# Tokens kept in float32 until they are turned, and cut into halves as the turned bank is emptied

## What is computed

```python
x = x + _L0_gnn_ref(_layernorm(x), adj, L0_gnn_W, L0_gnn_a)
x = x + _L0_ffn_ref(_layernorm(x), router_w, w1, b1, w2, b2)   # gelu, hidden 256
x = x + _L1_gnn_ref(_layernorm(x), adj, L1_gnn_W, L1_gnn_a)
x = x + _L1_ffn_ref(_layernorm(x), Wg, bg, bias, W1, b1, W2, b2)  # relu, hidden 512
# an expert layer: logits = t @ router; the best 2 of 8 experts; their weights w
# out = sum over the two of w_e * (act(t @ w1[e] + b1[e]) @ w2[e] + b2[e])  (layer 0 adds t)
```

## Time and profile before

| | us |
|---|---|
| median of 3 runs | 1315.85 (1315.29 to 1318.03) |
| the profiled execution | 1316.0 |
| its span, first to last instruction | 1314.2 |
| TensorE busy (products) | 1061.2, 81% |
| VectorE busy | 956.5, 73% |
| GpSimd busy | 706.3, 54% |
| ScalarE busy | 545.9, 42% |
| mean granted clock of TensorE | 0.882 |

### The profile page before, as it was taken

How to read it: one execution, slowest core, us unless ns; L and a number is a source line. 1 busy time by engine, 2 the same in 40 slices (tenths; PEclk the granted TensorE clock), 3 DMA queues, 4 the chain that set the end, 5 groups by cost and what they waited for, 6 DMA issues and landing times.

```text
span 1314.2 us, 31672 instructions
## 1 busy us (share of the span) xinstructions
PE 1061.2 (81%) x9392; PEld 888.3 (68%) x9393; DVE 956.5 (73%) x1904; ACT 545.9 (42%) x1223; POOL 706.3 (54%) x752
## 2 busy tenths in 40 slices
PE   6999765369999993477777587579999999899995
PEld 4777554258888883356555373368989987788984
DVE  5888898966777774469899787947766765666673
ACT  3666564912222221577777584112222232122221
POOL 4567657036666653778772281045443206777773
PEclk9999865569999997788879757689999999999998
DMA  9311233025555553336543464447776625444450
GB/s 284 79 49 41 81 113 128 1 65 163 165 161 166 166 160 119 92 104 171 151 137 104 138 200 119 28 131 221 205 223 183 173 78 155 126 136 134 139 144 21
DMA packets 126096, 172.53 MB, mean 131 GB/s; under 512 B 35109, under 2 KB 94000, under 8 KB 125744
## 3 DMA queue, kind: packets, MB, share of 16 engines
q0 software_dynamic: 28288, 83.03, 23.7%
q1 hardware_dynamic: 89504, 88.22, 21.3%
q10 hardware_dynamic: 8208, 0.07, 1.0%
HBM read 100.87 MB, written 71.44 MB: 131 GB/s over the span
## 4 chain that ended last, share of the span: by engine, by line
PE 48%; issue 18%; DVE 12%; POOL 12%; DMA 5%; ACT 3%; POOLq 0%; DVEq 0%; SPq 0%; ACTq 0%
PE bank L970 19%; PE bank L984 18%; POOL WREG L595 5%; PE bank L953 4%; PE bank L781 3%; DVE X L1306 2%; POOL X L678 2%; POOL WREG L643 2%; DMA WREG<-expert_outputs,pos_both 1%; DVE arena L1653 1%; ACT b_bc L1043 1%; DVE stats L1296 1%; DMA out<-X,scatter_row 1%; DMA X<-first_rows,gather_row 1%; DVE arena L1654 1%
## 5 line engine op out<-in xcount | busy, mean ns | idle before, releaser
L1205 ACT ACTIVATE arena<-bank,b1T 128x256 f32<-128x256 f32 (+1 forms) x464 | 176.4, 457 | 507.9 <-PE bank L970 507.8
L984 PE MATMUL bank<-WREG,arena 128*128 x2544 | 301.3, 273 | 16.4 <-issue 11.5
L970 PE MATMUL bank<-arena,WREG 128*128 128x256 f16 (+1 forms) x2784 | 311.7, 266 | 2.6 <-DVE arena L1717 2.6
L984 PEld LDWEIGHTS bank<-WREG,arena 128*128 128x128 f16 x2544 | 245.6, 98 | 53.0 <-issue 23.4
L970 PEld LDWEIGHTS bank<-arena,WREG 128*128 x2784 | 252.5, 99 | 32.2 <-issue 3.6
L1723 DVE CAST arena<-arena 128x1024 f16<-128x1024 f32 (+1 forms) x140 | 82.2, 587 | 192.1 <-ACT arena L1205 192.1
L667 POOL DMA_INDIRECT arena<-split_tokens,gather_row x136 | 134.9, 992 | 124.7 <-DVE gather_row L1694 47.1
L781 PE MATMUL bank<-wg_sb,arena 128*128 128x258 f32 x512 | 145.0, 433 | 47.2 <-ACT arena L1016 39.9
L595 POOL DMA_INDIRECT WREG<-expert_outputs,pos_both x128 | 127.5, 996 | 64.4 <-issue 36.8
L678 POOL DMA_INDIRECT X<-token_rows,gather_row x72 | 73.3, 1018 | 160.6 <-DMA first_rows<-X 67.4
L781 PEld LDWEIGHTS bank<-wg_sb,arena 128*128 128x128 f32 x512 | 105.6, 215 | 71.4 <-ACT arena L1016 41.7
(11 more groups left out here) (204 smaller groups left out, 1497.6 us busy)
## 6 DMA issues: line engine op xcount, KB each, us to landing
first_rows<-X SPq DMA_DIRECT2D x72, 257.0 KB, 4.3
expert_outputs<-arena SPq DMA_DIRECT2D x68, 256.0 KB
X<-in_x SPq DMA_DIRECT2D x16, 512.0 KB, 6.0
split_tokens<-WREG SPq DMA_DIRECT2D x16, 512.0 KB, 2.9
stage_w<-in_L_ffn_W SPq DMA_DIRECT2D x16, 512.0 KB, 4.8
token_rows<-X SPq DMA_DIRECT2D x8, 1024.0 KB, 7.2
token_rows<-WREG SPq DMA_DIRECT2D x16, 512.0 KB, 3.6
stage_w<-in_L_ffn_w SPq DMA_DIRECT2D x16, 256.0 KB, 2.8
```

The lines of the kernel that those rows point to most:

```text
L970: last = mm(hb, w1_at(L, ea, wh, kc, fc), tT[:, tb:tb + width], start=n == 0, stop=n == 3 * KC - 1)
L984: last = mm(ob[a], hsrc[:, h0:h0 + P], w2_at(L, e[a % len(e)], wh, fc), start=fc == 0 and n == 0, stop=fc == FC - 1 and n == 2)
L1205: ins = A(hid[:, h0:h0 + width], bank[2 + 2 * (u % 2) + fc // 2][:, b0:b0 + width], ACT.Gelu if L == 0 else ACT.Relu, bias=cut(b1T, ea * F ...
```

## The change

- `y32` is now 16 tiles long and takes the place of `y16`. Of each pair ScalarE scales the first tile (`normalise`) and VectorE the second (`cut_tokens`, a tensor_scalar). Nothing is cast or subtracted before the turn; GpSimd's loop is gone.
- SyncE stores `y32` itself. The bytes of a token are the same, 1024.
- TensorE turns four float32 blocks of 128 by 128 for a pair, and for a slot of the experts, in place of eight half-precision ones. They fill the bank with 512 float32 columns.
- ScalarE casts the bank to the upper part (512 columns), VectorE subtracts this from the bank for the lower part: `high_tokens` and `cut_tokens` in the token stage, `high_turned` and `low_turned` in the experts. `copy_yT` and `copy_T` are gone.
- In the experts' slots ScalarE casts slot s + 3 ahead of activating slot s + 2. Ahead of the loop its order is cast 0, cast 1, activate 0, cast 2, activate 1.
- Products, their order and the layout of `tT` stay; in `yT` only the order of blocks changes.

```diff
@@ buffers
-        y32, yT, y16 = ring0[:, 0:8 * D], ring0[:, 8 * D:12 * D].bitcast(F16), ring0[:, 16 * D:32 * D].bitcast(F16)
+        yT, y32 = ring0[:, 0:4 * D].bitcast(F16), ring0[:, 16 * D:32 * D]
@@ SyncE, stores
-                        sp.wait_ge(yl_ready[L], at(i * 8 + 2 * h + 2))
-                        y4 = y16[:, 4 * h * 512:(4 * h + 4) * 512]
+                        sp.wait_ge(y_ready[L], at(i * 8 + 2 * h + 2))
+                        sp.wait_ge(half_ready[L], at(i * 8 + 2 * h + 2))
+                        y4 = y32[:, 4 * h * D:(4 * h + 4) * D]
@@ GpSimd, the loop of the token stage
-                with pool.Fori(0, TILES // 16) as i:
-                    for q in range(8):
-                        loop_wait(pool, hi_ready[L], at(i * 8 + q + 1))
-                        nc.gpsimd.tensor_tensor(y16_4[:, 2 * q:2 * q + 2, D:2 * D], y32_4[:, 2 * (q % 4):2 * (q % 4) + 2, :],
-                                                y16_4[:, 2 * q:2 * q + 2, 0:D], ALU.subtract).then_inc(yl_ready[L], 1)
@@ TensorE, turn_tokens
-                    pe.wait_ge(yl_ready[L], at(i * 8 + q + 1))
+                    pe.wait_ge(y_ready[L], at(i * 8 + q + 1))
+                    pe.wait_ge(half_ready[L], at(i * 8 + q + 1))
                     yT_copied(pe, L, i, q - 2)
-                    for j in range(8):
-                        last = nc.tensor.transpose(bank[q % 2][:, j * (P // 2):(j + 1) * (P // 2)].bitcast(F16),
-                                                   y16[:, (8 * q + j) * P:(8 * q + j + 1) * P], ident16[:])
+                    for j in range(4):
+                        last = nc.tensor.transpose(bank[q % 2][:, j * P:(j + 1) * P], y32[:, (4 * q + j) * P:(4 * q + j + 1) * P], ident[:])
@@ TensorE, turn_over
-                    for j in range(4):
+                    for kc in range(KC):
                         for a in range(ST):
-                            last = nc.tensor.transpose(bank[u % 2][:, (j * ST + a) * (P // 2):(j * ST + a + 1) * (P // 2)].bitcast(F16),
-                                                       source[a][:, j * P:(j + 1) * P], ident16[:])
+                            last = nc.tensor.transpose(bank[u % 2][:, (kc * ST + a) * P:(kc * ST + a + 1) * P],
+                                                       source[a][:, kc * P:(kc + 1) * P], ident[:])
@@ ScalarE, normalise (one tile in place of two) and the cast
+                    p = i * 8 + q
+                    if q % 2 == 0:
+                        loop_wait(act, y_stored[q // 2][L], 16 + i * 16)
+                    loop_wait(act, yT_mm[L], at(p - 7))
+                    A(y32[:, 2 * q * D:(2 * q + 1) * D], xs(2 * p), ACT.Identity, scale=one("rs2", 2 * p), bias=one("nm2", 2 * p)).then_inc(y_ready[L], 1)
+                def high_tokens(i, q):
+                    p = i * 8 + q
+                    v = q % 2
+                    loop_wait(act, yT_mm[L], at(p + 1))
+                    loop_wait(act, logit_mm[L], at(p - 1))
+                    A(yT[:, v * 1024:v * 1024 + 512], bank[v][:], ACT.Copy).then_inc(yT_high[L], 1)
@@ ScalarE, the loop of the token stage
+                with act.Fori(1, TILES // 16) as i:
+                    for q in range(8):
+                        high_tokens(i, q - 3)
+                        normalise(i, q)
@@ ScalarE, experts
+                def high_turned(s, u):
+                    loop_wait(act, T_mm[L], at(s + 1))
+                    loop_wait(act, h_mm[L], at(s - 1))
+                    A(tT[:, (u % 2) * 4 * SLOT:(u % 2) * 4 * SLOT + KC * SLOT], bank[u % 2][:], ACT.Copy).then_inc(T_high[L], 1)
                 def slot(s, u, i, es):
+                    if u + 3 < SLOTS[L]:
+                        high_turned(s + 3, u + 3)
                     if u + 2 < SLOTS[L]:
                         activate(s + 2, u + 2, es[2])
-                for s in range(2):
-                    activate(s, s, first[s])
+                high_turned(0, 0)
+                high_turned(1, 1)
+                activate(0, 0, first[0])
+                high_turned(2, 2)
+                activate(1, 1, first[1])
@@ VectorE, cut_tokens
-                        loop_wait(dve, y_ready[L], at(p + 1))
-                        V.tensor_copy(y16_4[:, 2 * q:2 * q + 2, 0:D], y32_4[:, 2 * (q % 4):2 * (q % 4) + 2, :]).then_inc(hi_ready[L], 1)
-                    if not (first and q < 2) and (q - 2) % 4 != 3:
-                        loop_wait(dve, yT_mm[L], at(p - 1))
-                        loop_wait(dve, logit_mm[L], at(p - 3))
-                        V.tensor_copy(yT[:, v * 1024:(v + 1) * 1024], bank[v][:].bitcast(F16)).then_inc(yT_ev[L], 1)
+                        t = 2 * p + 1
+                        ts(y32[:, (2 * q + 1) * D:(2 * q + 2) * D], xs(t), one("rs2", t), one("nm2", t), ALU.mult, ALU.add).then_inc(half_ready[L], 1)
+                    if not (first and q < 2):
+                        loop_wait(dve, yT_high[L], at(p - 1))
+                        tt(yT[:, v * 1024 + 512:(v + 1) * 1024], bank[v][:], yT[:, v * 1024:v * 1024 + 512], ALU.subtract).then_inc(yT_ev[L], 1)
@@ VectorE, experts
-                def copy_T(s, u):
-                    loop_wait(dve, T_mm[L], at(s + 1))
-                    loop_wait(dve, h_mm[L], at(s - 1))
-                    V.tensor_copy(tT[:, (u % 2) * 4 * SLOT:(u % 2 + 1) * 4 * SLOT], bank[u % 2][:].bitcast(F16)).then_inc(T_ev[L], 1)
+                def low_turned(s, u):
+                    loop_wait(dve, T_high[L], at(s + 1))
+                    b = (u % 2) * 4 * SLOT
+                    tt(tT[:, b + KC * SLOT:b + 2 * KC * SLOT], bank[u % 2][:], tT[:, b:b + KC * SLOT], ALU.subtract).then_inc(T_ev[L], 1)
```

More of the change, by code:

```diff
@@ L667, in gather @@
                     nc.gpsimd.indirect_dma_start(
-                        out=gat[:, u * 512:(u + 1) * 512], out_offset=None, in_=table,
+                        out=gat[:, u * D:(u + 1) * D], out_offset=None, in_=table,
                         in_offset=bass.IndirectOffsetOnAxis(ap=gather_row[:, t:t + 1], axis=0)).then_inc(gathered[u // ST], 16)
@@ L1093, in normalise @@
                 def normalise(i, q):
-                    p = i * 4 + q
-                    loop_wait(act, yl_ready[L], at(p - 3))
-                    for a in range(2):
-                        t = 2 * p + a
-                        b = (2 * q + a) * D
-                        ins = A(y32[:, b:b + D], xs(t), ACT.Identity, scale=one("rs2", t), bias=one("nm2", t))
-                    ins.then_inc(y_ready[L], 1)
+                    p = i * 8 + q
[9 more added lines that the diff above has]
+                    A(yT[:, v * 1024:v * 1024 + 512], bank[v][:], ACT.Copy).then_inc(yT_high[L], 1)
                 for g in range(GROUPS):
@@ L1137, in _ @@
                         normalise(0, 3)
+                        high_tokens(0, 0)
                     if n < GROUPS and L == 1:
@@ L1146, in _ @@
                         squares(g + 2, 1)
-                def copy_yT(i):
-                    p = i * 4 - 1
-                    loop_wait(act, yT_mm[L], at(p + 1))
-                    loop_wait(act, logit_mm[L], at(p - 1))
-                    A(yT[:, 1024:2048], bank[1][:].bitcast(F16), ACT.Copy).then_inc(yT_act[L], 1)
-                def four_pairs(i):
-                    for q in range(3):
-                        normalise(i, q)
-                    copy_yT(i)
-                    normalise(i, 3)
-                four_pairs(1)
-                act.wait_ge(rs2_ready[L], at(2))
-                with act.Fori(2, TILES // 8) as i:
-                    four_pairs(i)
-                copy_yT(TILES // 8)
+                for q in range(4, 8):
+                    high_tokens(0, q - 3)
+                    normalise(0, q)
+                act.wait_ge(rs2_ready[L], at(2))
+                with act.Fori(1, TILES // 16) as i:
+                    for q in range(8):
+                        high_tokens(i, q - 3)
+                        normalise(i, q)
+                for q in range(-3, 0):
+                    high_tokens(TILES // 16, q)
                 def copy_low(j):
```

51 lines of the change are left out of this document (22 added, 29 removed).

## The result

The changed kernel takes 1319.62 us, the median of 11 runs (1316.91 to 1322.24), against 1315.29 us (1311.22 to 1318.03) for the kernel before in the same session. The ratio is 1.0033, with a 95% interval from 1.0021 to 1.0044. It is slower, by 4.3 us. The profiled execution has a span of 1318.4 us, before it was 1314.2, at a mean granted clock of 0.881 (0.882). One execution each of e3, of e10 and of the kernel before on the slower chip, 1.3 to 2 times as long as the others, stands in no median and no ratio here.

A forecast was written before the change was run, and what follows sets the result against it. TensorE was taken to bound the experts, a ring over two banks the token loop. Terms -2.3 - 0.5 - 1.2 + 1.0 - 1.0 + 2.2 + 1.3 sum to -0.5 us: 1315.4 us, no change, range 1305 to 1321.

The forecast's parts named there:

- The token loop: Token stage, both layers: steps fall from 1.45 and 1.42 us to 1.39, 26 per layer; -2.3 us.
- The ring: Token loop over two banks: turn, cast, subtraction, logits, turn after next; 2.78 us for two steps, 1.39 each.
- the new chain is no shorter: Rival, token loop: longer hand-overs and address issue on VectorE make steps 1.45; 1319.6 us with starts at upper bounds; chance 0.15.
- The scaling on VectorE: Token loop: VectorE's scaling of one tile per pair takes 0.28 us, at most about 0.42.
- The ends: Token loop's first turn after the statistics (-0.48) and last turn's way to the logits (+0.24); -0.5 us for both layers.
- Routing without GpSimd: Layer 0's routing arithmetic, no longer beside GpSimd's one-hot tables and last expert's weights; -1.2 us.
- GpSimd beside the last attention group: Layer 0: moved GpSimd work may delay the last softmax's product; cost between 0 and 1.16, taken as +1.0 us.
- The float32 turn in the experts: Experts' slots: four float32 turns take 0.43 us against 0.45 for eight half-precision ones; taken as -1.0 us.
- The rival of a load for each block: Rival, float32 turn: each block costs a whole load, 141 ns; 1330 us, a third of it 1321; chance 0.15.
- The start of the experts: First output products come later behind ScalarE's order: layer 0 +2.2 (0.6 to 2.9), layer 1 +1.3 us (0.6 to 2.5).
- The clock rival: Rival, token loop: TensorE's clock stays up, step 1.15 us; 1302.9 us, or 1309 in half the loop; chance 0.2.

The follow-up runs named there:

- e3: Changed kernel with ScalarE's first expert activation right behind its first cast and VectorE's first split ahead of its third subtraction; 1393.32 us on a slower chip, ratio 1.0015.
- e10: Changed kernel, still looped, but a turn in TensorE's token loop waits only for the subtraction two pairs back; 1314.19 us, ratio 0.9980.
- e4: Changed kernel with TensorE's token loop written out; 1379.74 us on a slower chip, ratio 0.9937 to the kernel before.
- e6: Kernel before with TensorE's token loop written out and nothing else; 1316.01 us, ratio 1.0003.
- e11: Changed kernel with one more wait, so GpSimd makes layer 0's tables and last weights late, beside routing again; 1322.78 us, ratio 1.0050.
- e9: The changed kernel's experts, float32 table and float32 turn behind the token stage of the kernel before; 1313.40 us, ratio 0.9981.
- e5: The changed kernel itself, run again on a second chip; 1320.32 us, ratio 1.0035 to the kernel before.
- e7: Changed kernel with the start order of e3 and, in layer 0, an early one-column Gelu that loads the table; 1318.19 us, ratio 1.0023.
- e12: Changed kernel with logits two turns behind, the edits of e4 and e10, and the early one-column Gelu of e7; 1294.88 us, ratio 0.9843.
- e8: Changed kernel with logits two turns behind and the edits of e4 and e7; 1311.88 us, ratio 0.9959.

## Why the prediction was wrong

I gave 1315.4 us and called it no change; 1319.6 came, 4.3 slower than before, where I had said that 2.6 can be told apart. It lies inside my range of 1305 to 1321 only because two misses partly cancel: the token loop came 9.5 us above its term, and the experts, +2.5 with their starts, came out at about -2.5. The first miss alone gives 1324.9. That the range held is luck. In the order of its steps:

- **The token loop, -2.3.** This is the step that failed; +7.2 was measured (40.61 - 37.72 + 41.19 - 36.88). The ring was named rightly, and two of its operations were right to 0.01: cast 0.60, subtraction 0.69. The mis-sized terms are TensorE's: 0.28 from the logits to the next turn was 0.44, the turn 1.09 in place of 1.03, and the end of TensorE's loop, 0.50 once in eight steps, was not in the sum at all. The hand-overs were right in sum only, 0.22 for my 0.20: 0.16 behind VectorE and 0.03 behind the two others. Together these make the step 1.52 without the loop's end and 1.56 to 1.58 with it, in place of 1.39. The 0.28 was the shortest such leg of the kernel before, and it holds the products and loads alone. I took for granted that waits already met are free, because in the kernel before they are: they lie under the wait for GpSimd. The change took that cover away and added a wait. e4, e6 and e10 show it from three sides.
- **The rival "the new chain is no shorter"** was the nearest, and had 1319.6 as its time, which is what came. But that is chance. It put the issue on VectorE, and it was TensorE's; the step was 1.56 to 1.58, not 1.45; and the experts paid part of it back, where this rival had their starts at the upper bounds. It had 0.15. The rule I would use now would have given it more: a cycle that was never on the path has unpriced legs.
- **The scaling on VectorE** took 0.41 in the loop, its upper bound of 0.42, not 0.28. It cost nothing in the ring: the subtraction still began 0.03 behind the cast.
- **The ends, -0.5.** The first turn came 1.3 and 1.4 us after the statistics in place of 1.8 and 1.9, as forecast; the last turn's way to VectorE's routing grew by 0.4 in place of 0.24.
- **Routing without GpSimd, -1.2.** Last turn to rank products went from 13.80 to 12.71, the 0.4 above included, so 1.1 net and 1.5 for the arithmetic. e11 puts it back. **GpSimd beside the last attention group, +1.0:** not seen in the loop's start. The softmax product L1379 (L1381 before) took 0.69, as alone, though it began under GpSimd's iota, which has no input and ended 0.29 after the product's start (rows below). By the Trainium skill, SBUF — State Buffer, section "SBUF: two separate sides", the pair of ports is locked against such a VectorE operation only by a GpSimd operation that reads SBUF. The trace agrees with that as far as it goes: 0.69 here, and 1.85 for the same line beside a GpSimd subtraction. The multiply behind the iota, which reads SBUF, met the rest of the product and took 1.83 itself, with a median of 1.49. I had read the rule without its condition.

```profile
152.55 3.15 POOL L601 IOTA arena<- 128x256 bf16 x2
...
155.41 0.69 DVE L1379 TENSOR_TENSOR arena<-arena,soft_cols 128x512 f32<-128x512 f32 x1
...
155.68 1.83 POOL L568 TENSOR_SCALAR stage_w<-stage_w 128x512 f32<-128x512 f32 x1
```

- **The float32 turn in the experts, -1.0.** Slots of layer 1 went from 5.69 to 5.68 us (twelve slots from 1206.44 to 1274.56), the turn is 0.44. The rival of a load for each block is out: a float32 load takes 143 ns here, and it hides (0.44 from turn to product). e9 gives the whole experts' part 2.5 us under the kernel before, though its start is late. How much of that is the 0.01 a slot in about 128 slots (1.3) and how much falls from waits for gathered rows, no run separates; it stays open.
- **The start of the experts, +2.2 and +1.3.** First turn to first output products grew by 2.7 and 2.2, within the bounds (3.0 and 1.5 in e5). In layer 0 the cause is as forecast, ScalarE's one queue of casts, table and activation: e7 took 1.0 to 1.3 off by moving the table. For layer 1 no run shows it; another order there was no better. That it would be kept to the end was wrong, by e9.
- **The clock rival** (0.2) did not come about in the change. In e12, where the clock did rise after the ring was cut, a step at the upper clock took 1.08 us, near its price of 1.15.

## What to carry to other kernels

Before an engine's wait is taken out of a loop, look at what that engine's queue does in it: semaphore waits, register arithmetic and the loop's end cost nothing under it and stand in the ring when it is gone. Count those instructions on the engine that closes the ring, drop waits that another wait implies, and write the loop out if its steps are near a microsecond. A work split that is even over the engines is worth little as long as the cycle of dependences, not an engine, sets the step.

## What was not expected of the hardware

- In TensorE's queue a semaphore wait that stands alone has a record of 51 ns, register arithmetic for it 32 ns, a computed address 64 ns; but two such waits in a row start 106 ns apart. Two waits in a ring of two steps were worth 2.2 to 2.4 us a layer (e10). The Trainium skill, Advanced Engine Details and Errata, section "Network/Comms", puts reading a semaphore from the sequencer at 50 to 100 ns on this chip; if a wait that is met is such a read, the 51 ns agree with its lower end and the 106 ns lie just above it.
- The end of TensorE's loop took 0.50 us between products (0.94 for 0.44).
- TensorE's clock rose in the middle of the token loop in e12 (0.50, 0.62, 1.00 in three stretches) with TensorE busy 9.1 to 9.3 of 10 us before it rose. In e8, busy up to 9.2 of 10 us, it stayed at 0.50 in layer 0's loop and was up in layer 1's only from about 777.7 to 781; in the kernel before it was up for about 3.7 us in either loop. No run here shows what decides it.
- A float32 turn of four blocks costs TensorE as much as the half-precision one of eight at the upper clock, 0.44 us against 0.45; at the lower clock the records give 1.09 against 1.03.
